# An attention and convolution kernel on one core: the image loop written out, two adds of short slots on GpSimd, pairs of maxima in odd units

## The reference

```
x = x + attention(group_norm(x))      # layer 0
x = x + masked_conv(group_norm(x))    # layer 1

attention: t = x as (B, 1024 tokens, 512)
  q, k, v = t @ W.T + b, reshaped to (B * 8, 1024, 64)
  softmax(q @ k.T / 8) @ v
```

## Time and profile before

| what | us |
|---|---|
| median of 3 runs (2628.47 to 2631.73) | 2628.54 |
| the profiled execution, its own time | 2624.4 |
| its span, from the first to the last instruction | 2622.4 |
| TensorE busy | 2457.1 |
| VectorE busy | 1934.6 |
| ScalarE busy | 1149.1 |
| GpSimd busy | 1097.6 |

### The profile page before, as it was taken

The page is one execution under the profiler, slowest core; times in us unless marked ns, Lnnn a source line. Parts: engine busy times, 40 slices in busy tenths (PEclk is TensorE's granted clock), DMA queues, the critical chain, the costliest instruction groups (busy, mean ns, idle before and its releaser), DMA issues.

```text
span 2622.4 us, 43917 instructions
## 1 busy us (share of the span) xinstructions
PE 2457.1 (94%) x13768; PEld 912.8 (35%) x13768; DVE 1934.6 (74%) x2645; ACT 1149.1 (44%) x2059; POOL 1097.6 (42%) x970
## 2 busy tenths in 40 slices
PE   6899899989989999998999999998999999999999
PEld 2233233323323333332333333332344444444444
DVE  5787778768768877877877788986766966967515
ACT  4455455545545555554564555457332132132100
POOL 1465466546546645653664665565103012021000
PEclk9999999999999999999999999999999999999999
DMA  3213222131322213132221323223443644633534
GB/s 125 75 47 85 72 80 81 43 97 47 88 73 86 72 42 104 40 88 90 69 81 33 103 71 104 73 67 101 153 143 135 242 150 150 245 133 141 192 99 174
DMA packets 162830, 268.47 MB, mean 102 GB/s; under 512 B 80160, under 2 KB 80288, under 8 KB 162592
## 3 DMA queue, kind: packets, MB, share of 16 engines
q1 hardware_dynamic: 162320, 264.41, 31.3%
q10 hardware_dynamic: 272, 1.05, 0.1%
HBM read 195.54 MB, written 52.69 MB: 95 GB/s over the span
## 4 chain that ended last, share of the span: by engine, by line
PE 78%; DVE 11%; issue 5%; ACT 2%; DMA 2%; POOL 1%; DVEq 0%; SPq 0%; ACTq 0%; POOLq 0%
PE bank L845 28%; PE bank L750 14%; PE bank L724 12%; PE bank L675 11%; PE bank L685 6%; DVE nmax L1277 6%; PE bank L696 4%; DVE prob_sum L1270 2%; ACT prob L927 2%; PE bank L706 1%; DMA q_top<-shift 1%; DVE val L1289 1%; DVE bn L222 1%; PE bank L737 0%; DVE den_sb L1298 0%
## 5 line engine op out<-in xcount | busy, mean ns | idle before, releaser
L1277 DVE TENSOR_REDUCE nmax<-bank 128x1 f32<-128x512 f32 x1024 | 647.0, 680 | 268.7 <-PE bank L696 252.7
L927 ACT ACTIVATE prob<-bank 128x512 f32<-128x512 f32 x1024 | 560.9, 593 | 554.3 <-PE bank L724 554.3
L845 PE MATMUL bank<-v,u_slab 128*128 128x512 f16 x3456 | 746.9, 379 | 0.0
L1107 POOL TENSOR_TENSOR prob_sum<-prob_sum,prob 128x512 f32<-128x512 f32 x354 | 481.9, 1361 | 387.2 <-ACT prob L927 386.9
L750 PE MATMUL bank<-prob,val 128*64 128x512 f32 x2048 | 503.6, 612 | 11.4 <-issue 6.3
L845 PEld LDWEIGHTS bank<-v,u_slab 128*128 128x128 f16 x3456 | 338.1, 98 | 406.9 <-issue 0.8
L1270 DVE TENSOR_TENSOR prob_sum<-prob_sum,prob 128x512 f32<-128x512 f32 x354 | 333.4, 942 | 3.2 <-DVE val L1289 0.2
L696 PE MATMUL bank<-k_hi,q_hi 64*128 64x512 f16 x1024 | 200.6, 387 | 61.1 <-DVE nmax L1277 47.5
L724 PE MATMUL bank<-q_hi,k_hi 64*128 64x512 f16 x1024 | 197.6, 382 | 43.4 <-ACT prob L927 43.0
L750 PEld LDWEIGHTS bank<-prob,val 128*64 128x64 f32 x2048 | 126.7, 137 | 251.5 <-issue 212.2
L675 PE MATMUL bank<-xn_hi,w_hi 128*128 128x512 f16 x512 | 196.1, 383 | 7.8 <-DVE xn_lo L1254 7.8
(11 more groups left out here) (145 smaller groups left out, 2848.2 us busy)
## 6 DMA issues: line engine op xcount, KB each, us to landing
u_slab<-u_scratch SPq DMA_DIRECT2D x72, 1024.0 KB, 5.0
xs<-x SPq DMA_DIRECT2D x28, 1024.0 KB, 5.4
tile<-x_scratch SPq DMA_DIRECT2D x26, 1024.0 KB, 6.9
u_scratch<-u_w SPq DMA_DIRECT2D x96, 192.0 KB, 2.7
den_sb<-recip_scratch SPq DMA_DIRECT2D x128, 128.0 KB, 2.9
x_scratch<-xr SPq DMA_DIRECT2D x16, 1024.0 KB, 4.9
xr<-x SPq DMA_DIRECT2D x15, 1024.0 KB, 8.0
res<-x_scratch SPq DMA_DIRECT2D x14, 1024.0 KB, 8.8
```

The source lines that it names most:

```text
L845: mm = pe.matmul(bank_at(pos, co)[:].rearrange("p (i n) -> p i n", i=2), slab[:, l, c, co * P:(co + 1) * P], image[v][:, 2 * c:2 * c + 2, ...
L927: act.activation(prob[:, (2 * u + e) % 8], sc_bank[bank_turn(s * 16 + 2 * u + e, 16 * HPI)[0]][:], ACT.Exp, scale=float(D) ** -0.5).then_i ...
L1107: nc.gpsimd.tensor_tensor(acc, in0, prob[:, (2 * kc + 1) % 8], ALU.add).then_inc(s1["sum1"], 1)
L1277: dve.tensor_reduce(nmax[:, seg, part:part + 1], src[:], AX.X, ALU.max, negate=True)\
```

## The change

It has three parts.

1. The loop over images is an ordinary Python loop on all five engines: the six passes are written out in the program, and all numbers waited for are constants. `Count` shrinks to a counter.
2. In short slots (r = 3) that use the two sums, the even adds of kc = 2 and kc = 5 are done by GpSimd (`add_even`), right before its own odd add of the same kc, with the same semaphores; VectorE skips them.
3. `MAX_AT` has two tables. Short slots, and slots of the last image that project nothing, keep the old one. Slots with projections have pairs 2 and 5 after the scores of units 1 and 3, ahead of the projection of that unit, and pairs 3 and 6 before the scores of units 2 and 4.

```diff
-MAX_AT = {(0, "a"): 0, (1, "a"): 1, (2, "a"): 2, (2, "c"): 3, (3, "a"): 4, (4, "a"): 5, (4, "c"): 6, (5, "a"): 7}
+MAX_AT = ({(0, "a"): 0, (1, "a"): 1, (2, "a"): 2, (2, "c"): 3, (3, "a"): 4, (4, "a"): 5, (4, "c"): 6, (5, "a"): 7},
+          {(0, "a"): 0, (1, "a"): 1, (1, "c"): 2, (2, "a"): 3, (3, "a"): 4, (3, "c"): 5, (4, "a"): 6, (5, "a"): 7})
+EVEN_BY_POOL = (2, 5)
...
-def ring_items(u, nxt, prev, v_units, stat):
-
-    at = {place: [("max", MAX_AT[u, place])] if nxt and (u, place) in MAX_AT else [] for place in "ac"}
+def ring_items(u, nxt, prev, v_units, stat, proj):
+
+    at = {place: [("max", MAX_AT[proj][u, place])] if nxt and (u, place) in MAX_AT[proj] else [] for place in "ac"}
...
                 if ring.n >= ago:
-                    pe.wait_ge(s1["ring_free"], ring.value() + 3 - ago)
+                    pe.wait_ge(s1["ring_free"], ring.n + 3 - ago)
...
-            with pe.Fori(0, B - 2) as i:
-                ring.loop(i)
+            for i in range(B - 2):
                 for s in range(1, HPI):
                     slot(i, s)
                 slot(i + 1, 0)
-            ring.done(B - 2)
...
+            def add_even(h, s, kc):
+                pool.wait_ge(s1["exp_done"], 4 + 16 * h + 2 * kc + 1)
+                acc = psum_acc[:, s % 2, 0]
+                pool.wait_ge(s1["sum0"], 7 + 7 * h + kc - 1)
+                nc.gpsimd.tensor_tensor(acc, acc, prob[:, (2 * kc) % 8], ALU.add).then_inc(s1["sum0"], 1)
+
...
                     if u >= 2 and not den_direct(s, more):
+                        if s % HPH == 3 and u - 1 in EVEN_BY_POOL:
+                            add_even(h, s, u - 1)
                         add_tile(h, s, u - 1)
...
-                        if place == "d" and u >= 2 and not den_direct(s, more):
+                        if place == "d" and u >= 2 and not den_direct(s, more) and not (r == 3 and u - 1 in EVEN_BY_POOL):
                             add_tile(h, s, u - 1)
```

More of the change, by code:

```diff
@@ L71, with __init__ @@
 class Count:
[L74 to L85, removed]
+    def __init__(self):
+        self.n = 0
 def bank_turn(n, period, banks=3):
@@ L218, in sync @@
             def sync():
-                dve.wait_ge(signal, step.value())
+                dve.wait_ge(signal, step.n)
             def moments(k, half, src):
@@ L559, in _ @@
             slot(0, 0, prev=False)
-            with sp.Fori(0, B - 2) as i:
+            for i in range(B - 2):
                 for s in range(1, HPI):
@@ L636, in _ @@
         def _(pe):
-            ring = Count(PER_RING)
+            ring = Count()
             def take():
@@ L767, in slot @@
                     items = ring_items(u, nxt, "direct" if den_direct(s - 1, more) else prev, proj and r == 2,
-                                       stat_units(s, more))
+                                       stat_units(s, more), proj)
                     def run(place):
@@ L1061, in _ @@
             slot(0, 0, prev=False)
-            with act.Fori(0, B - 2) as i:
+            for i in range(B - 2):
                 for s in range(1, HPI):
@@ L1213, in _ @@
             slot(0, 0, prev=False)
-            with pool.Fori(0, B - 2) as i:
+            for i in range(B - 2):
                 for s in range(1, HPI):
@@ L1234, in _ @@
         def _(dve):
-            ring = Count(PER_RING)
-            step = Count(STAT_STEPS)
+            ring = Count()
+            step = Count()
             def item():
-                dve.wait_ge(s1["ring_full"], ring.value() + 1)
+                dve.wait_ge(s1["ring_full"], ring.n + 1)
                 src = v_ring[bank_turn(ring.n, PER_RING)[0]]
@@ L1243, in item @@
                 return src
-            step2 = Count(0)
+            step2 = Count()
             moments, aggregate, centre, finish = statistics(dve, s_stat, step, NC)
@@ L1279, in max_item @@
                 if m == 15:
-                    dve.wait_ge(s1["ring_free"], 2 + ring.value())
+                    dve.wait_ge(s1["ring_free"], 2 + ring.n)
                     dve.tensor_tensor(nmin[:, 0:SEG], nmax[:, :, 0], nmax[:, :, 1], ALU.min).then_inc(s1["min_done"], 1)
@@ L1319, in first_pair_stat @@
                 (centre2, finish2)[k](src, s1["ring_free"])
-            mstep = Count(0)
-            vstep = Count(0)
-            ystep = Count(0)
+            mstep = Count()
+            vstep = Count()
+            ystep = Count()
             def chain(ins):
@@ L1677, in _ @@
             slot(0, 0, prev=False)
-            with dve.Fori(0, B - 2) as i:
-                ring.loop(i)
-                step.loop(i)
+            for i in range(B - 2):
                 for s in range(1, HPI):
@@ L1683, in _ @@
                 slot(i + 1, 0)
-            ring.done(B - 2)
-            step.done(B - 2)
             for s in range(1, HPI):
```

## The result

| what | before | after |
|---|---|---|
| median, us | 2628.51 (2625.31 to 2631.73, 4 runs) | 2591.31 (2586.64 to 2596.92, 4 runs) |
| ratio, 95% interval | | 0.9859 [0.9836, 0.9883] |
| profiled execution, its own time | 2624.4 | 2592.32 |
| its span | 2622.4 | 2590.5 |

What follows compares the result with a forecast made beforehand. TensorE, busy 94%, was taken as the bound. Loop 39 plus adds 7 minus pairs 4 gave 42 us off the 2628.5 median: 2586.5, stated as 2586, own range 2577 to 2594 (chance 0.47), whole range 2561 to 2606.

Steps and rivals of the forecast that it cites:

- the one slot 0 that no branch follows: Last loop pass: its slot 0 takes 28.97 us, used as slot 0's price in straight code, against 33.21 before a branch.
- waits on constants: Loop written out: ring and statistics waits become constant; 0.1 us taken off each of slots 3 to 7 and 0.
- starved fetch: Rival, chance 0.03: TensorE's instruction fetch falls behind in straight code, gaps appear inside slots; 115 us slower, 2743.
- The rival that GpSimd holds VectorE up: Chance 0.08: GpSimd's added work delays VectorE's adds, so 7 us gained becomes 16.5 lost; 2609 (2600 to 2614).
- The sign that I gave for it: VectorE's adds: their mean was to fall below 942 ns if the order helps.
- The argument from the order: Slot 3: GpSimd's odd add of tile 2 now follows VectorE's first add, so the 16.5 us loss was not taken.
- the 0.43 us in front of one pair: Slot 3, unit 4: second pair of maxima comes 1.37 us after the scores' start, not 0.94; moving tile 2's add returns this.
- only VectorE's adds can lose: Port sharing with GpSimd: maxima read PSUM and are free, so only VectorE's adds stretch, 16.5 us at worst.
- VectorE has only pair 1 there, so its first maximum is done in time: Unit 1, slots with projections: the moved pair was to find its bank free, with no new wait.
- my 0.3 to 1.2: Slots 2 and 6, unit 3: us of new wait expected from the moved pairs.
- The wait in unit 3 that I named: TensorE waits for pair 4's maximum, which VectorE takes late: 0 to 0.7 us, in slot 0 0.7 to 1.6.
- one of my signs of being wrong: Prediction wrong if slot 0 stays above 31, slots with projections move over 1 us, or GpSimd's adds stretch.

Runs made afterwards that it cites:

- the first move alone: Whole change, but in slots with projections only pairs 2 and 3 moved, pairs 5 and 6 back at old places: 2587.00 us, 0.9834 of the kernel before.
- the second alone: Whole change, but in slots with projections only pairs 5 and 6 moved, pairs 2 and 3 back at old places: 2631.37 us, one run.

## Why the prediction was right

**The loop.** Predicted 39 us, six passes of 1317.3; the kernel with the loop alone has passes of 1317.5 (39.1 less) and a median 41 us lower. What carried it was to price the branch back by the one slot 0 that no branch follows, and not by the issue gaps alone: those sum to 18.4 us, less than half. The trace of the kernel before gives the rest. At the five edges TensorE also waits 5.1 us for exponentials that come late (1.90, 2.31 and 0.85), and the granted clock is at its lower level for 6.8 us at four edges and 3.4 at the fifth; TensorE is busy for 22.3 of these 30.6 us, with work that takes half of that at the higher level. That makes 18.4 + 5.1 + 11.1 = 34.6, an estimate from these rows, against 33 us in slot 0. Slot 0 had 33.2 to 36.6 us in five images and has 28.9 in all, 33 us in sum. One detail was wrong: slots 4 and 5 did not gain from waits on constants (28.85 to 28.87), slots 2 and 6 gained 0.15 each; that constants are the reason there is not shown, since no run had the loop without them. No starved fetch appeared: TensorE's list of waits for the passes has no issue line left, so that rival falls.

**The adds.** Predicted 7 us, measured 10 in the medians and 14 x 0.6 = 8 in the slots. Tile 2 gives all of it and tile 5 nothing, as predicted. The rival that GpSimd holds VectorE up is false. The sign that I gave for it, the mean of VectorE's adds, was badly chosen: it rose from 942 to 1030 ns, while VectorE's adds as a whole fell by 28.5 us (16.0 against the kernel with the loop alone), and GpSimd's odd adds stayed nearly as they were (1361 and 1373 ns). The argument from the order held: the first add of slot 3 takes 0.68 us and not 1.56. But I took the gain from the 0.43 us in front of one pair, and never counted that first add; that 0.5 a slot came out near 0.6 is in part luck. The Trainium skill's rule (SBUF — State Buffer, "Who interferes with whom") bore on more than adds: the split, which has two SBUF inputs too, stretched from 0.69 to 1.75 us beside GpSimd, while the maxima kept 682 ns. I had not counted the splits, and where I wrote that only VectorE's adds can lose, they belong there too.

**The pairs.** The sign was right and the size off: 4 us slower predicted, 10 measured. By slots (gains positive): slot 0 -0.3 predicted, -0.42 measured; slot 4 -0.1 to +0.3 and slot 5 -0.5 to 0 predicted, +0.05 each measured; slot 6 +0.5, measured -0.04; slot 2 -0.3, measured -0.4 to -1.1. Slot 1 -0.2 predicted, -0.5 measured on its shortest: a wait of 1.30 us for a maximum has come in unit 3, where one of 0.45 in unit 4 went, and it isn't hidden behind the row of shifts, since the row itself is issued 0.49 us later (23.33 instead of 22.84 us behind the mark). The steps that were mis-sized are those of slots 1, 2 and 6. I wrote that in unit 1 "VectorE has only pair 1 there, so its first maximum is done in time", which is false in slot 2: a split of 1.76 us stands ahead of it, and the waits of unit 1 come to 0.4 to 1.1 us. Unit 3 came to 1.15 in slots 2 and 6 alike, the upper end of my 0.3 to 1.2. And what the move removes is 1.2 to 1.3 us of waits there, not 1.7. In slot 6 the first move alone loses 0.25 and the second alone gains 0.46, and together they don't add up. The wait in unit 3 that I named is the cause of the second move's cost in slots 0, 4 and 5, as the kernels with one move show.

**The sum.** 2591.3 against 2586, inside the forecast's own range. It came so near because errors cancelled: the loop and the adds gave 2 and 3 us more than predicted, the pairs took 6 more, and that is luck. The profiled execution, for which the sum was made (2582.4), took 2592.3. The parts alone give 41 + 10 - 10 = 41, the whole change 37. The 4 us between are within what these medians can tell. The late row of shifts was not in my working at all; it took 5 us in the profiled execution's first image, and the runs of the whole change spread over 10 us. That the pairs cause it is not borne out: it also came in kernels without them (33.75 us with the add of tile 5 alone), and the kernel with loop and pairs had no wait for the row above 0.6 us. It also answers one of my signs of being wrong: slot 1 of the first image moved by 5.3 us (31.74 to 37.04), and the clock was at its lower level behind it, where I had forecast the higher one throughout.

## What to carry to other kernels

A loop on the chip can be priced from its own trace, by a pass that no branch follows: here the five branches back cost 33 us in slot 0 alone, 6.7 each, and straight code of 48 slots ran without an issue gap above 0.15 us. Moving work to a second engine paid here where it stood ahead of the item that TensorE waits for, and not otherwise, though the work moved was as long. The mean of one group of instructions shifts when members leave it or change places, so compare the sum over all such groups, or single places. An order that suits one kind of slot has to be tried for each kind by itself; and a small transfer that the next step needs is better issued before a large one that nobody waits for yet.

## What the runs showed that I had not expected

- The branch back costs more than its two waits: TensorE's clock was granted at 0.50 for the stretch behind it, and the product in it took 3.78 us where it takes 1.94.
- Two rows of 1 KB took up to 8 us from their issue to their use behind a load of 1 MB, in the slot in which both were issued late.
- A single wait of 2 us on TensorE in slot 0 was followed by the lower clock in five of six cases, at a price of 1.7 us each on top of the wait, and one of 2.39 us in slot 1 of the same kernel in none of seven.
